# Fifteen batches' projections, values, output products and input turns as 64-row products, seven PSUM places by a table, and new orders of work

## What is computed

```python
x = _layernorm(x + _L0_attn_ref(x, w_qkv, w_proj))                  # 16 heads of 16, rotary, softmax over 512 keys
x = _layernorm(x + _L0_xattn_ref(x, ctx, ctx, Wq, bq, ... Wo, bo))  # 16 heads of 16, keys and values from ctx
x = _layernorm(x + _L0_ffn_ref(x, ...))                             # two layers of windowed attention and gated MLP

# inside _L0_ffn_ref, for each of 2 layers, (b, n, 256) seen as 8 heads of 64, windows of 128 tokens
h = shift_token(x); q, k, v = split(h @ wqkv)
q, k = rotary_xpos(l2norm(q) * qs, l2norm(k) * ksc)
x = x + softmax(mask(q @ k.T over this window and the one before)) @ v @ wo
h = layernorm(shift_token(x)); a, g = split(h @ w1 + b1)
x = x + (a * gelu(g)) @ w2 + b2
```

## Time and profile before

| | |
|---|---|
| median of 3 runs | 2189.59 us (2188.16 to 2189.70) |
| the profiled execution | 2188.94 us, its span 2187.2 us |
| PE busy, x matmuls | 2092.9 us (96%), x13992 |
| PE weight loads | 1472.3 us (67%) |
| DVE / ACT / POOL busy | 1669.8 (76%) / 1498.5 (69%) / 1330.7 (61%) |
| mean granted TensorE clock | 0.982 of full |
| score products (L594) | x1024, 386.4 us busy |
| maximum products (L579) | x1024, 361.8 us busy |
| PV products (L610) | x2048, 269.5 us busy |
| maxima on DVE (L1004) | x1024, 641.4 us busy, 682 ns each |
| exponentials on ACT (L829) | x1024, 555.1 us busy, 603 ns each |

### The profile page before, as it was taken

The page is one execution under the profiler, slowest core; times in us unless marked ns, Lnnn a source line. Parts: engine busy times, 40 slices in busy tenths (PEclk is TensorE's granted clock), DMA queues, the critical chain, the costliest instruction groups (busy, mean ns, idle before and its releaser), DMA issues.

```text
span 2187.2 us, 44568 instructions
## 1 busy us (share of the span) xinstructions
PE 2092.9 (96%) x13992; PEld 1472.3 (67%) x13992; DVE 1669.8 (76%) x3989; ACT 1498.5 (69%) x3418; POOL 1330.7 (61%) x1378
## 2 busy tenths in 40 slices
PE   4999999999999999879999999999899999999997
PEld 3544444444444444357888887788778888887887
DVE  5888788888888888558888887565488888875775
ACT  2388788888888888736777777544377777775443
POOL 2444466443445444668888886464378887875775
PEclk8799999999999999989999999999999999999999
DMA  4124333433333333435554544200155555551211
GB/s 131 59 93 128 103 108 109 122 105 111 116 110 115 120 120 115 138 87 148 109 120 107 111 105 115 67 20 6 56 108 114 114 111 108 112 121 44 64 58 44
DMA packets 191072, 216.13 MB, mean 99 GB/s; under 512 B 24128, under 2 KB 117056, under 8 KB 190848
## 3 DMA queue, kind: packets, MB, share of 16 engines
q1 hardware_dynamic: 188288, 204.90, 35.3%
q0 software_dynamic: 2560, 8.39, 1.0%
HBM read 47.14 MB, written 29.89 MB: 35 GB/s over the span
## 4 chain that ended last, share of the span: by engine, by line
PE 88%; DVE 3%; POOL 3%; SPq 2%; ACT 2%; issue 2%; DMA 1%; POOLq 0%; ACTq 0%; DVEq 0%
PE PS L491 15%; PE PS L492 13%; PE PS L493 13%; PE PS L610 11%; PE PS L594 11%; PE PS L579 7%; PE PS L703 5%; PE PS L679 5%; PE PS L688 4%; PE PS L663 2%; SPq L1464 1%; PE PS L586 1%; ACT PT L829 1%; PE PS L527 1%; PE PS L635 1%
## 5 line engine op out<-in xcount | busy, mean ns | idle before, releaser
L1004 DVE TENSOR_REDUCE MX<-PS 128x1 f32<-128x512 f32 x1024 | 641.4, 682 | 145.3 <-PE PS L579 138.1
L829 ACT ACTIVATE PT<-PS 128x512 f32<-128x512 f32 x1024 | 555.1, 603 | 124.1 <-PE PS L594 122.6
L594 PE MATMUL PS<-QS,KS 64*128 64x512 f32 x1024 | 386.4, 455 | 6.1 <-ACT PT L829 5.3
L579 PE MATMUL PS<-KS,QS 64*128 64x512 f32 x1024 | 361.8, 451 | 17.5 <-DMA KS<-HL 15.8
L594 PEld LDWEIGHTS PS<-QS,KS 64*128 64x128 f32 x1024 | 166.2, 185 | 270.2 <-issue 137.0
L1373 POOL TENSOR_TENSOR PB<-PB,RC 128x512 f32<-128x512 f32 (+1 forms) x256 | 250.3, 997 | 48.5 <-DVE RC L1126 48.5
L610 PE MATMUL PS<-PT,VP 128*17 128x512 f32 x2048 | 269.5, 598 | 1.3 <-ACT OT L836 0.6
L890 ACT ACTIVATE PB<-PB,NMf 128x256 f32<-128x256 f32 (+1 forms) x512 | 242.5, 477 | 8.5 <-DVE NMf L1117 8.4
L579 PEld LDWEIGHTS PS<-KS,QS 64*128 64x128 f32 x1024 | 173.1, 189 | 72.8 <-issue 40.9
L1353 POOL TENSOR_TENSOR RI<-RI,mhalf 128x8 f32<-128x8 f32 x128 | 213.3, 1667 | 10.7
L1117 DVE CUSTOM_DVE_ANT_0 PB<-PS,mk 128x256 f32<-128x256 f32 (+1 forms) x512 | 175.7, 385 | 53.7 <-PE PS L679 53.5
(11 more groups left out here) (186 smaller groups left out, 5158.3 us busy)
## 6 DMA issues: line engine op xcount, KB each, us to landing
qT<-QN SPq DMA_DIRECT2D x384, 128.0 KB
kT<-kT SPq DMA_DIRECT2D x256, 128.0 KB
od<-OT SPq DMA_DIRECT2D x64, 256.0 KB, 2.7
QS<-HL SPq DMA_DIRECT2D x96, 128.0 KB
KS<-HL SPq DMA_DIRECT2D x96, 128.0 KB
QS<-HL SPq DMA_DIRECT2D x48, 256.0 KB
KS<-HL SPq DMA_DIRECT2D x48, 256.0 KB
OC<-od SPq DMA_DIRECT2D x32, 256.0 KB
```

The source lines that it names most:

```text
L579: pe.matmul(PS[:, bank, :], QS[rows, s, h // 2, qt * P:(qt + 1) * P], KS[rows, s, h // 2, :], start=True, stop=True).then_inc(fills("amax" ...
L594: pe.matmul(PS[:, bank, :], KS[rows, s, pair, kt * P:(kt + 1) * P], QS[rows, s, pair, :], start=True, stop=True).then_inc(fills("score", v ...
L829: act.activation(PT[:, kt % 2, 2 * i + half], PS[:, TURNS["score", vb, g, kt, half, i][0], :], ACT.Exp).then_inc(drains("score", vb, g, kt ...
L1004: dve.tensor_reduce(MX[:, vb % 2, h // 8, qt, c:c + 1], PS[:, TURNS["amax", vb, h, qt][0], :], AX, ALU.max).then_inc(drains("amax", vb, h, ...
```

## The change

In the 16-head part, for the virtual batches 1 to 15 (batch 0's turns and projections and the last batch's output product stay whole):

- `rope`, `bias1`, `val` and `proj` become products of 64 rows: the upper half of the contraction goes into one bank and the lower half into another at the same time, and in a second step the two halves change banks, so that each bank ends with the full sum. A stage that was "tile 0, then tile 1" is now "step 0, then step 1"; both banks are taken before step 0 and both are filled at the end of step 1. Step 1 waits on a new semaphore (`crossed_...`) until step 0's last two products are done. The number of columns streamed is the same; the number of instructions doubles.
- `tr` becomes turns of 64 rows x 128 into 128 x 64, in two steps, in the same way.
- What waited for the second tile's bank now waits for both (`tr_hi`, `ctx_hi`, `add_bo`, `load_w`, `spread`, `load_consts`).
- The seven banks other than 3 are one pool for scores, maxima and everything else, and a table `BANKS` (2,239 digits, one for each use) says which is taken.
- `SELF_ORDER`, `CROSS_ORDER` and `WINDOW_ORDER` have new places; window code is otherwise unchanged.

```diff
 SELF_ORDER = (
-    (1, "out_lo", (0,), 3), (2, "val", (0,), 0), (4, "ot", (3,), 2), (5, "val_out", (0,), 0), (5, "val_out", (1,), 0), (5, "val", (1,), 0),
...
+    (0, "ot_out", (3,), 2), (2, "val", (1,), 0), (4, "sums", (), 2), (4, "val_out", (0,), 0), (4, "val_out", (1,), 0), (5, "tr", (0,), -1),
...
 WINDOW_ORDER = (
-    ("wsum", 1, -1), ("wval", None, -1), ("wpt", 0, 1), ("wrot", 1, -1), ("woh", None, 2), ("wpt", 1, 1), ("wout", None, 2), ("wres", None, 2),
...
+    ("wval", None, -1), ("wpt", 0, 1), ("wscale", 2, 1), ("wout", None, 2), ("wqk", 0, -2), ("wscore", 0, 0), ("wqn", 1, -1), ("wqkh", 0, -1),
...
+CROSSED = ("rope", "bias1", "val", "proj", "tr",)
+WHOLE = {"rope": 4, "tr": 2}
...
+BANKS = (
+    "01245670124561274052761405214076540726154072615407261540726154072615407276154027615476154716450246075142076154675146257267526750"
...
 def bank_turns(stages):
...
-        elif kind in ("tr", "rope", "bias1", "val", "maxtr", "proj", "amax", "fold"):
-            use(s, 4 + ring[0] % 4)
-            ring[0] += 1
-        elif kind == "score":
-            use(s, ring[1] % 3)
-            ring[1] += 1
+        elif kind in CROSSED and not (kind in WHOLE and a[0] == 0):
+            for k in range(2 if a[-1] == 0 else 0):
+                use(s[:-1] + (k,), int(next(banks)))
...
+        elif kind in ("tr", "rope", "bias1", "val", "maxtr", "proj", "amax", "fold", "score"):
+            use(s, int(next(banks)))
...
+            def crossed(kind, *stage):
+                pe.wait_ge(sem["crossed_" + kind], nth(kind, *stage) - WHOLE.get(kind, 0))
+
+            def project_rows(kind, vb, qk, step):
+                if step:
+                    crossed(kind, vb, qk, 1)
+                for kc in range(2):
+                    for n, (a, b) in enumerate(((0, 0), (0, 1), (1, 0))):
+                        for r, rows in enumerate(HALVES):
+                            tile, last = step ^ r, kc == 1 and n == 2
+                            m = pe.matmul(PS[:, TURNS[kind, vb, qk, tile][0], :], W[rows, kc, a, qk, tile * P:(tile + 1) * P], xT[rows, kc, b],
+                                          start=step == kc == n == 0, stop=step == 1 and last)
+                            if last:
+                                m.then_inc(fills(kind, vb, qk, tile) if step else sem["crossed_" + kind], 1)
...
+            def val(vb, step):
                 weights_ready(int(vb >= NB), 2)
...
                 for i in range(2):
-                    tok = slice((2 * half + i) * P, (2 * half + i + 1) * P)
                     for kc in range(2):
-                        m = terms(PS[:, bank, i * D:(i + 1) * D], (xT[:, kc, 0, tok], xT[:, kc, 1, tok]),
-                                  (W[:, kc, 0, 2], W[:, kc, 1, 2]), pe, kc == 0, kc == 1)
-                m.then_inc(fills("val", vb, half), 1)
+                        for n, (a, b) in enumerate(((0, 0), (0, 1), (1, 0))):
+                            for r, rows in enumerate(HALVES):
+                                half, last = step ^ r, i == kc == 1 and n == 2
...
```

176 lines of the change are left out of this document (128 added, 48 removed).

## The result

| | before | after |
|---|---|---|
| median | 2189.57 us (2188.16 to 2189.70, 4 runs) | 2136.83 us (2133.34 to 2138.61, 4 runs) |
| profiled execution, span | 2188.94, 2187.2 us | 2138.61, 2136.8 us |
| mean granted clock of the profiled execution | 0.982 | 0.974 |

The ratio is 0.9759, 95% interval 0.9742 to 0.9776: faster by 52.7 us, where 66.4 were forecast (2123 us).

The account below looks back on a forecast made before the run. TensorE bounds the kernel except in PV periods without side work. Terms -41.0 - 1.6 - 3.0 + 4.2 - 2 - 23 = -66.4 against 2188.94 give 2122.5; the median's 0.65 makes 2123 us, range 2094 to 2166.

Parts of the forecast that it names:

- (1) borders: 16-head part: half-row pairs remove 0.39 us borders around 105 groups, -41.0 us, and part of them at eight behind PV, -1.6.
- eight pairs of loads x 0.11, nothing: Input turns as 64-column pieces: eight pairs of loads at 0.11 us, as eight loads before; no change.
- The pair of 256 columns, 0.119: Value and output groups: a half-row pair of 256 columns takes 0.119 us, as a whole product did; change 0.
- (2) crossing wait: Second steps wait for the first step's last products; covered by two pairs between, 0; uncovered some 0.3 us each, 23 us.
- (3) maxima turns before PV: 15 of 31 maxima turns now stand right before PV and need one border less each way: -3.0 us.
- (4): Where groups stand: PV periods without side work go from 114 to 123 of 254, at 0.47 us each, +4.2 us.
- (5) places by a table: Seven pooled places in the 16-head part: taken as 0, bounds 0 or -58 us, since VectorE would stop the period anyway.
- places run short: Rival, chance 0.09: steps holding two of seven places make TensorE wait; +30 us (2153), or with two waits 2182.
- (6) start: Before the first score: one value group moves ahead of the wait for the first rows, -2 us.
- (7) windows: Window part: two PV groups per window become one, 64 visits fewer at 0.36 us each, -23 us.
- smoothed surplus: Rival, chance 0.14: more places let VectorE catch up behind projections, half of the 58 us, giving 2094.
- serial loads: Rival, chance 0.07: both halves' weight loads run one after the other, 256-column pairs take 0.22 us, total 2211.

Follow-up runs that it names:

- experiment 6: Changed kernel with values and output products again as whole 128-row products, table and order kept; 2151.67 us, ratio 0.9821.
- experiment 4: Changed kernel with VectorE's maxima reading only 256 of the 512 key columns; 2131.95 us.
- experiment 7: Changed kernel with the input turns again as whole 128-row transposes; 2137.12 us, ratio 0.9758.
- experiment 10: Changed kernel with ScalarE's value copies, from the third batch on, of one head of 16 instead of all; 2132.22 us, ratio 0.9750.
- experiment 9: Changed kernel with the second step of each value and output pair directly behind its first, in one period; 2172.11 us, ratio 0.9934.
- experiment 5: Changed kernel with seven places by a simple rule, a quad's four scores in four places, and VectorE's maxima reading 256 of 512 columns; 2242.21 us.
- experiment 2: Changed kernel with places by a simple rule instead of the table: scores only in 0, 1, 2, all else in 4 to 7; 2316.06 us.
- experiment 3: Changed kernel with all seven places by a simple rule instead of the table, a quad's four scores in four different places; 2288.24 us.
- experiment 8: Changed kernel with the window part's weight and constant loads, and the casts reading them, later in the drain's list; 2133.41 us, ratio 0.9740.
- experiment 11: Changed kernel with later window loads and the last but one batch's output casts moved from places 55 and 56 to 59; 2131.63 us, ratio 0.9749.
- experiment 1: Kernel before with the new window order and nothing else; 2166.06 us, ratio 0.9888.

## Why the prediction was right, and by how much not

The time, 2136.83 us, lies in the range (2094 to 2166) and on the side given 0.90. By the prediction's own steps:

- **(1) borders, -41.0 and -1.6.** Right in mechanism and price. The periods with values, outputs and single projections in cross steps lost 0.37 to 0.39 each; for values and outputs experiment 6 put it back, for projections it rests on the periods alone. What failed is the sum: the step took TensorE for the bound in *every* period with side work ("in a period with projections TensorE is the bound"). In self steps it is not in the turn period and the one behind it: there ScalarE and VectorE are (experiments 4, 7, 10), and the borders taken away there are worth nothing. I had the earlier trace rows only for a bare period, and no row of the two reader engines in a turn period.
- **The turns, "eight pairs of loads x 0.11, nothing".** Mis-sized: four pairs take 0.22 us, 0.055 each, half of the forecast's price. It changes nothing in the time (experiment 7), because the period is not TensorE's. A price from the row of 128-column loads was not the price of a 64-column turn.
- **The pair of 256 columns, 0.119.** Exact. 24 instructions in 1.43 us are 0.060 each, and the 16 of a group in the earlier trace rows pass at 0.053. The Trainium skill (TensorE: Matmul & The Clock Gate, Wait — 56ns, not 53.3ns?) gives 62 ns per MATMUL for the case that hardware decode is off, which would have made it 0.124; no trace here says which case this is, and both rows are faster than that figure.
- **(2) crossing wait, 0.** Right, and its price without cover, 0.3, measured as 0.33 (experiment 9). What I did not see is that the distance between the two steps does more than cover this wait: it spreads the side work over two periods' slack. Of experiment 9's 38.6 us between the PVs some 9 (27 x 0.33) are the wait, the rest is this.
- **(3) maxima turns before PV, -3.0.** Not seen: a period with maxima turns alone takes 2.93 for 2.94 on average (2.84 to 2.88 for 2.91 in twelve of them, 3.13 to 3.25 in four). It too has a surplus that is not TensorE's, 2.12 + 0.53 being 2.65, so a border less is worth next to nothing in it. **(4)** The bare periods stayed what they were, 2.64 for 2.62, so nine more of them cost what was counted.
- **(5) places by a table, 0.** Right in number, for half the reason. The loop of the fourth score is the bound of 92 bare periods, and in the 20 without it VectorE stops the period, at 2.72 (experiments 4, 5). But experiments 2 and 3 put +151 to +179 us on a table made by a simple rule, which is outside the forecast's rival "places run short" (+30, +60): its mechanism was the right one, its worst price three times too small. In the changed kernel it does not happen.
- **(6) start, -2.** It came to -6.2. The count of borders began with the first PV and left out the groups that stand among maximum products before it, nine in the trace of before: 9 x 0.39 = 3.5, and with the 2 that is 5.5. This is a count, not a test, and experiment 6 speaks against it: there three of these groups (values) are whole again and the first PV starts at 88.0, no later than the 88.5 of the changed kernel. Four executions that do the same up to there (the changed kernel, 8, 10, 11) start it from 87.0 to 89.3 us. So why the start gained 4 us more than forecast stays open.
- **(7) windows, -23.** Right: -23.4 alone. Window by window it is 0.33 for the 0.36 of the sum, since the one visit that is left costs some 0.5 where it now stands; a full window takes 11.8 to 12.5 us, depending on its place among the four, not 12.15 throughout.

The forecast says 16 PVs in 51.3 (self) and 51.0 (cross) and measures 52.2 to 52.9 and 51.4 to 51.9. In the profiled executions 16.0 us are missing: 15.0 between first and last PV, 3.4 in the stretch with the MLP of layer 0, 2.0 in the window part, less 4.2 gained more at the start and 0.2 in the rest. The total is closer than its terms, since the start's surplus hides part of what the 16-head part lacks; that is luck. The profile's sign of being wrong "TensorE waiting for VectorE or ScalarE on a place right before or behind a group" did appear, in the turn periods of self steps (0.20 us for VectorE at 244.58). Of the rivals none came true; "smoothed surplus" is out by the bare period of 2.59, serial loads by 0.119, the windows by -23.4. The one that was missing is "the readers bound the periods around the turns".

The 3.4 us stand at the border from the MLP to the second layer, where the 16-head part plays no role but the new `WINDOW_ORDER` does. The stretches, of the kernel before:

```profile
1530.00:1609.00 79.00, 68.07 (x401) 57.10 (x401) 42.15 (x104) 34.37 (x76) 38.79 (x36) 0.98 0.31 78
```

and of the changed one:

```profile
1486.00:1569.00 83.00, 73.65 (x401) 61.80 (x400) 42.12 (x100) 33.45 (x76) 37.54 (x35) 0.88 0.28 69
```

The same 401 instructions in 79 and in 83 us, at a granted clock of 0.98 and 0.88. In both TensorE waits a few times for 0.7 to 1.9 us there. In pieces of 5 us the granted clock falls to 0.71 once before, and after it is 0.50 (that is 1.2 GHz) from 1525 to 1530, behind two waits of 1.5 and 1.6 us, and 0.50 and 0.60 from 1550 to 1560, amid waits of 1.5 and 1.0. Is it chance or the new window order? All twelve profiled kernels with that order, experiment 1 among them, take 234.0 to 236.8 us from the last WOF group of layer 0 to the first product of layer 1, where the kernel before takes 232.8, and the granted clock in the last 79 us is 0.87 to 0.96 for 0.98 (experiment 1: 235.9 us and 0.91; experiment 7: 234.0 and 0.94). So it is not peculiar to this execution: some 1 us stands in every one, and up to 3 us more come and go, mostly with a lower clock. There is only one profile of the kernel before, so that the order causes it is likely but not shown. The medians compare executions with all of this in them.

## What to carry to other kernels

Count borders between array shapes as instructions with a price, here 0.39 us for a group of whole products among half-row ones, but credit the price only in periods where TensorE is the bound: before summing, look at each *kind* of period, with every engine's work in it, because the kinds that differ are the few that decide how much of a regular gain arrives. Side work put one piece to a period hides in the slack of each; two pieces in one period use one slack and starve the other engines. And more PSUM places are worth nothing by their number: the same seven were worth 150 us more by a good assignment than by a simple rule (one execution each, and part of it a lower clock).

## What the runs showed that was not expected

- Turns of 64 rows and 64 columns in pairs pass at 0.055 us a pair, whole turns of 128 at about 0.15 each (0.58 for four with the border).
- The bounds of a bare period lie close together: 2.59 (place loop), 2.72 where VectorE holds it, and 2.45 us with both away. Removing one shows next to nothing in the total, and experiment 4 alone would have read as "VectorE does not matter".
- A step that accumulates in a place where the other row half has just written, and that the program holds back by a semaphore until those products are done, starts 0.33 us late when it follows at once, and not at all late with two pairs between.
- Which place a product writes to moved the time by 7 to 8% (one execution each), with the same instructions in the same order.
